# Sparsemax thresholds from Newton steps on the candidates instead of a sort, and a rolled exact loop

## What is computed

```
xn   = layernorm(x);  q = xn@Wq + bq;  k = ctx@Wk + bk;  v = ctx@Wv + bv
s    = q k^T / sqrt(32)                  # per head, 100 x 722
p    = sparsemax(s)                      # max(s - tau, 0), tau such that each row sums to 1
x1   = x + (p v)@Wo + bo
x2n  = layernorm(x1)
y    = x1 + sqrt((x2n@cos(theta+theta_noise))^2 + (x2n@sin(phi+phi_noise))^2)
```

## Time and profile before

| | us |
|---|---|
| median of 3 runs | 852.85 |
| lowest, highest | 851.33, 861.3 |
| span of the profiled execution | 858.3 |
| VectorE busy in it | 639.5 (75%) |
| TensorE busy | 681.9 (79%) |
| ScalarE busy | 480.7 (56%) |
| GpSimd busy | 195.8 (23%) |

### The profile page before, as it was taken

One profiled execution on the slowest core, in us unless ns is written; L12 is line 12 of the kernel. 1 busy time (PEld: TensorE's weight loads), 2 busy tenths in 40 slices (PEclk: granted clock), 3 DMA queues, 4 the chain that ended last, 5 costly groups with the idle time before them and its releaser, 6 DMA issues.

```text
span 858.3 us, 17053 instructions
## 1 busy us (share of the span) xinstructions
PE 681.9 (79%) x5152; PEld 441.6 (51%) x5152; DVE 639.5 (75%) x4046; ACT 480.7 (56%) x936; POOL 195.8 (23%) x147
## 2 busy tenths in 40 slices
PE   3895843879977789899889988988949898986485
PEld 3562522645555454665467455855437455742351
DVE  2799995599936997499929994799638995899401
ACT  3271754655485554875388546765537566843441
POOL 4940450001520034102520162004410053000000
PEclk9898885979989799899989999999969999998687
DMA  7620100000020000200020002000020000000000
GB/s 233 247 99 1 68 3 1 2 2 1 11 90 1 0 10 1 90 0 0 10 91 0 0 10 67 24 0 10 1 86 4 0 10 11 3 1 10 11 3 10
DMA packets 14576, 26.27 MB, mean 31 GB/s; under 512 B 2106, under 2 KB 2106, under 8 KB 14478
## 3 DMA queue, kind: packets, MB, share of 16 engines
q1 hardware_dynamic: 14478, 25.35, 8.9%
HBM read 23.71 MB, written 1.64 MB: 30 GB/s over the span
## 4 chain that ended last, share of the span: by engine, by line
DVE 71%; issue 9%; PE 7%; DMA 5%; DVEq 3%; SPq 3%; ACT 2%; ACTq 0%; POOL 0%; POOLq 0%
DVE cand L772 22%; DVE cand L784 17%; DVE top L779 14%; DMA xq<-in_x 3%; PE tps L438 3%; DVE csum L794 2%; PE work L422 2%; DMA out_y<-att 2%; DVE x L871 2%; DVE gk L797 2%; DVE topz L790 1%; DVE g_max L800 1%; SPq L197 1%; DVE st L747 1%; PE work L342 1%
## 5 line engine op out<-in xcount | busy, mean ns | idle before, releaser
L772 DVE MAX8 cand<-S 100x8 f32<-100x60 f32 (+1 forms) x1536 | 191.0, 208 | 49.0 <-ACT S L576 28.7
L438 PE MATMUL tps<-ident,S 100*128 100x100 f32 x768 | 106.0, 282 | 82.3 <-DVEq L864 47.5
L422 PE MATMUL work<-kT,qz 128*100 128x361 f16 x768 | 153.8, 342 | 0.8 <-ACT k_f L597 0.8
L613 ACT ACTIVATE S<-S,neg_tau 100x722 f32<-100x722 f32 x128 | 115.0, 900 | 68.2 <-DVE neg_tau L802 68.2
L287 POOL TENSOR_TENSOR ctxT<-ctxT_f,ctxT 128x1024 f16<-128x1024 f32 x24 | 54.0, 2248 | 426.5 <-ACT ctxT_f L576 426.5
L784 DVE MATCH_REPLACE8 cand<-top,cand 100x96 f32<-100x96 f32 x640 | 149.1, 250 | 0.0
L337 PE MATMUL work<-wv,ctxT 128*128 128x512 f16 x576 | 130.8, 384 | 19.8 <-ACT v L576 19.4
L779 DVE MAX8 top<-cand 100x8 f32<-100x96 f32 x768 | 141.2, 252 | 0.0
L438 PEld LDWEIGHTS tps<-ident,S 100*128 100x128 f32 x768 | 87.0, 158 | 104.0 <-ACT pT L576 45.5
L337 PE MATMUL work<-ctxT,wk 128*128 128x361 f16 x768 | 128.3, 329 | 10.8 <-ACT k_f L597 9.1
L576 ACT ACTIVATE S<-work 100x722 f32<-100x722 f32 x128 | 99.6, 778 | 33.0 <-PE work L422 30.8
(11 more groups left out here) (102 smaller groups left out, 671.4 us busy)
## 6 DMA issues: line engine op xcount, KB each, us to landing
ctx_nat<-in_ctx SPq DMA_DIRECT2D x8, 1280.0 KB
xq<-in_x SPq DMA_DIRECT2D x8, 200.0 KB
xr<-in_x SPq DMA_DIRECT2D x8, 200.0 KB
out_y<-att SPq DMA_DIRECT2D x8, 200.0 KB
ctx_nat<-in_ctx SPq DMA_DIRECT2D x8, 164.0 KB
wq<-in_L_xattn_Wq SPq DMA_DIRECT2D x1, 1024.0 KB, 7.4
S<-in_L_xattn_Wk SPq DMA_DIRECT2D x1, 1024.0 KB, 9.5
S<-in_L_xattn_Wv SPq DMA_DIRECT2D x1, 1024.0 KB, 11.2
```

The source lines that it names most:

```text
L422: last = nc.tensor.matmul(buf[0:L, half, 0:HALF], qz2[:, i, h // G, h % G, :], kT2[:, j, h // G, half * HALF:(half + 1) * HALF], start=(n ...
L438: last = nc.tensor.transpose(tps[:, half, c * L:(c + 1) * L], S[0:L, h, kc * P:(kc + 1) * P], ident[0:L, 0:L])
L613: nc.scalar.activation(S[0:L, h, 0:N], S[0:L, h, 0:N], ACT.Relu, bias=neg_tau[:, h:h + 1], accum_out=row_sum[:, h:h + 1]).then_inc(relu_do ...
L772: last = nc.vector.max(cand[:, j, 8 * i:8 * i + 8], S[0:L, h, cuts[i]:cuts[i + 1]])
```

## The change

`thresholds` becomes two parts. `maxes(b, g)` is a generator that issues the MAX8 of a group one by one, into one of two `cand` buffers. `sparse_tau(g, between)` takes tau by Newton steps for the four heads at once: the start is (sum of the two largest of each piece - 1)/24, which is not above the true tau; each step takes the differences of the first 4, 6, 8 and 8 ranks of each piece to tau, counts those that are not negative (as bf16 zeros and ones, halved in width by one addition before the reduce), sums the positive ones, and adds (sum - 1)/count to tau. Between its dependent operations `between(n)` issues n MAX8 of the next group, and all that are left at its end; for group 3 there are none. So group 3's MAX8 are now ahead of `tail1`. The semaphore counts are cleared once a pass.

`settle` copies the eight counts as integers and their maximum; if that isn't zero, a loop over the eight heads loads each count into a register and has one If with one `refine`, whose arrays are addressed by the loop's register. The 57 small memsets of the two tables at the start go.

```diff
-TOP = 48
 PIECES = 12
+RANKS = (4, 6, 8, 8)
 NEWTON_MAX = 28
-LOWEST = -3.0e38
...
-        cand = sb("cand", [L, G, NCAND])
-        top = sb("top", [L, G, TOP])
-        topz, csum, gk = (sb(n, [L, G, TOP]) for n in ("topz", "csum", "gk"))
-        chain0, inv_k = sb("chain0", [L, G, TOP]), sb("inv_k", [L, G, TOP])
-        g_max = sb("g_max", [L, G])
+        cand = sb("cand", [L, 2, G, NCAND])
+        dif, over = sb("dif", [L, G, NCAND]), sb("over", [L, G, NCAND], BF16)
+        tau_t, f_sum, count_g, inv_g = (sb(n, [L, G]) for n in ("tau_t", "f_sum", "count_g", "inv_g"))
+        zero = sb("zero", [L, 1])
...
-        scratch = cand[:, :, :].rearrange("p g n -> p (g n)").bitcast(BF16)[:, 0:N]
+        scratch = dif[:, :, :].rearrange("p g n -> p (g n)").bitcast(BF16)[:, 0:N]
...
-            def thresholds(b, g):
-
-                base = step = 0
-
+            def maxes(b, g):
 
                 dve.wait_ge(s_ready, H * b + G * (g + 1))
                 dve.sem_inc(scores_seen, 1)
-                dve.sem_clear(find)
-                dve.sem_clear(tau_step)
                 for j in range(G):
-                    h = G * g + j
                     for i in range(PIECES):
-                        last = nc.vector.max(cand[:, j, 8 * i:8 * i + 8], S[0:L, h, cuts[i]:cuts[i + 1]])
-                    last.then_inc(find, 1)
...
+                        last = nc.vector.max(cand[:, g % 2, j, 8 * i:8 * i + 8],
+                                             S[0:L, G * g + j, cuts[i]:cuts[i + 1]])
+                        if i == PIECES - 1:
+                            last.then_inc(found, 1)
+                        yield
+
+            def sparse_tau(g, between):
+
+                n = tau_count[0]
+                pieces = cand[:, g % 2, :, :].rearrange("p g (i r) -> p g i r", r=8)
+                dve.wait_ge(found, G * (g + 1))
+                nc.vector.tensor_reduce(f_sum[:, :], pieces[:, :, :, 0:2], mybir.AxisListType.XY,
+                                        ALU.add).then_inc(tau_step, 1)
+                between(4)
+                dve.wait_ge(tau_step, n + 1)
+                nc.vector.tensor_scalar(tau_t[:, :], f_sum[:, :], -1.0, 1.0 / (2 * PIECES), ALU.add,
+                                        ALU.mult).then_inc(tau_step, 1)
+                n += 2
+                for ranks in RANKS:
+                    E = PIECES * ranks
+                    d4 = dif[:, :, 0:E].rearrange("p g (i r) -> p g i r", r=ranks)
+                    t4 = tau_t[:, :].rearrange("p (g a c) -> p g a c", a=1, c=1)
+                    between(1)
+                    dve.wait_ge(tau_step, n)
+                    nc.vector.tensor_tensor(d4, pieces[:, :, :, 0:ranks],
+                                            t4.broadcast_to([L, G, PIECES, ranks]),
+                                            ALU.subtract).then_inc(tau_step, 1)
+                    between(1)
+                    dve.wait_ge(tau_step, n + 1)
+                    nc.vector.tensor_scalar(over[:, :, 0:E], dif[:, :, 0:E], 0.0, None, ALU.is_ge)\
+                        .then_inc(tau_step, 1)
+                    nc.vector.tensor_scalar(dif[:, :, 0:E], dif[:, :, 0:E], 0.0, None, ALU.max).then_inc(tau_step, 1)
+                    dve.wait_ge(tau_step, n + 2)
+                    nc.vector.tensor_tensor(over[:, :, 0:E // 2], over[:, :, 0:E // 2], over[:, :, E // 2:E],
+                                            ALU.add).then_inc(tau_step, 1)
+                    dve.wait_ge(tau_step, n + 3)
+                    nc.vector.reduce_sum(f_sum[:, :], dif[:, :, 0:E], AX).then_inc(tau_step, 1)
+                    dve.wait_ge(tau_step, n + 4)
+                    nc.vector.reduce_sum(count_g[:, :], over[:, :, 0:E // 2], AX).then_inc(tau_step, 1)
+                    between(1)
+                    dve.wait_ge(tau_step, n + 6)
+                    nc.vector.tensor_scalar(count_g[:, :], count_g[:, :], 1.0, None, ALU.max).then_inc(tau_step, 1)
+                    between(1)
+                    dve.wait_ge(tau_step, n + 7)
+                    nc.vector.reciprocal(inv_g[:, :], count_g[:, :]).then_inc(tau_step, 1)
+                    between(1)
+                    dve.wait_ge(tau_step, n + 8)
+                    nc.vector.scalar_tensor_tensor(f_sum[:, :], f_sum[:, :], -1.0, inv_g[:, :], ALU.add,
+                                                   ALU.mult).then_inc(tau_step, 1)
+                    between(1)
+                    dve.wait_ge(tau_step, n + 9)
+                    nc.vector.tensor_tensor(tau_t[:, :], tau_t[:, :], f_sum[:, :], ALU.add).then_inc(tau_step, 1)
+                    n += 10
+                between(1)
+                dve.wait_ge(tau_step, n)
+                nc.vector.tensor_scalar(neg_tau[:, G * g:G * (g + 1)], tau_t[:, :], -1.0, None,
+                                        ALU.mult).then_inc(tau_ready, 1)
+                tau_count[0] = n
+                between(G * PIECES)
+
+            def filler(of):
+
+                def between(n):
+                    for _ in range(n):
+                        next(of, None)
+                return between
...
             def refine(h):
 
+                p = S[0:L, bass.ds(h, 1), 0:N].rearrange("p a n -> p (a n)")
                 dve.sem_clear(fix)
-                n = newton(h, 0, row_sum[:, h:h + 1])
-                n = newton(h, n, new_sum[:, :])
+                n = newton(p, 0, row_sum[:, bass.ds(h, 1)])
+                n = newton(p, n, new_sum[:, :])
...
-                nc.vector.tensor_scalar(flag_bits[:, :], flag_ps, 0.5, None, ALU.is_gt).then_inc(check_step, 1)
-                dve.wait_ge(check_step, 1)
-                nc.vector.scalar_tensor_tensor(flag_bits[:, :], flag_bits[:, :], 1.0, bit[:, :], ALU.mult, ALU.mult,
-                                               accum_out=flag_code[:, :]).then_inc(check_step, 1)
+                nc.vector.tensor_copy(flag_i[:, :], flag_ps).then_inc(check_step, 1)
+                nc.vector.reduce_max(any_i[:, :], flag_ps, AX).then_inc(check_step, 1)
                 dve.wait_ge(check_step, 2)
-                nc.vector.tensor_copy(flag_i[:, :], flag_code[:, :]).then_inc(check_step, 1)
-                dve.wait_ge(check_step, 3)
-                todo = dve.value_load(flag_i[0:1, 0:1], min_val=0, max_val=2 ** (2 * G) - 1)
+                todo = dve.value_load(any_i[0:1, 0:1], min_val=0, max_val=L)
                 with dve.If(todo > 0):
-                    for n in range(2 * G):
-                        with dve.If((todo >> n) & 1 > 0):
-                            refine(2 * G * part + n)
+                    with dve.Fori(0, 2 * G) as n:
+                        rows = dve.value_load(flag_i[0:1, bass.ds(n, 1)], min_val=0, max_val=L)
+                        with dve.If(rows > 0):
+                            refine(n + 2 * G * part)
...
-                thresholds(b, 0)
-                thresholds(b, 1)
-                thresholds(b, 2)
+                dve.sem_clear(found)
+                dve.sem_clear(tau_step)
+                tau_count[0] = 0
+                none = filler(iter(()))
+                filler(maxes(b, 0))(G * PIECES)
+                sparse_tau(0, filler(maxes(b, 1)))
+                sparse_tau(1, filler(maxes(b, 2)))
+                sparse_tau(2, filler(maxes(b, 3)))
                 if not first:
                     tail1(b - 1)
                 mark(b, 0)
-                thresholds(b, 3)
+                sparse_tau(3, none)
                 if not first:
                     sum_squares(b - 1)
                 settle(b, 0)
```

More of the change, by code:

```diff
@@ L156, in build_kernel @@
         att_ready, x1_ready, res_ready = (sem(n) for n in ("att_ready", "x1_ready", "res_ready"))
-        find, tau_step, check_step, fix = sem("find"), sem("tau_step"), sem("check_step"), sem("fix")
         scores_seen = sem("scores_seen")
+        found, tau_step, check_step, fix = sem("found"), sem("tau_step"), sem("check_step"), sem("fix")
         ln1_stat, ln1_sd, ln1_step, xn_ready = (sem(n) for n in ("ln1_stat", "ln1_sd", "ln1_step", "xn_ready"))
@@ L758, in ln1 @@
                            ln1_stat, ln1_sd, ln1_step, xn_ready)
-            def thresholds(b, g):
-                base = step = 0
+            def maxes(b, g):
                 dve.wait_ge(s_ready, H * b + G * (g + 1))
                 dve.sem_inc(scores_seen, 1)
-                dve.sem_clear(find)
-                dve.sem_clear(tau_step)
                 for j in range(G):
-                    h = G * g + j
                     for i in range(PIECES):
-                        last = nc.vector.max(cand[:, j, 8 * i:8 * i + 8], S[0:L, h, cuts[i]:cuts[i + 1]])
-                    last.then_inc(find, 1)
[L774 to L782, removed]
-                            dve.wait_ge(find, base + n - G + j + 1)
-                            nc.vector.match_replace(cand[:, j, :], top[:, j, 8 * r:8 * r + 8], cand[:, j, :],
-                                                    LOWEST).then_inc(find, 1)
```

(27 more changed lines are left out.)

10 lines of the change are left out of this document (4 added, 6 removed).

## The result

The changed kernel takes 875.6 us (median of 4; 873.22 to 879.74), the one before 852.09 (median of 4 by now): a ratio of 1.0267, 95% interval 1.0223 to 1.031. It is slower.

A forecast was written before the change was run, and what follows sets the result against it. VectorE was taken to bound the kernel. Six steady passes +8, first pass +1.7, three flagged settles +19.5 and last pass -6.3 gave +23 us on the median 852.85: 876 us, 8-in-10 range 842 to 902.

The forecast's parts named there:

- the two paths: Steady pass: x2n to TensorE's FFN and k projections; fourth threshold to sum_squares and ScalarE's root, relus and k copies.
- Two points set the pass: VectorE, steady pass: only when x2n is out (T+54.5) and when sum_squares runs (T+71.6) matter.
- The chain's price: VectorE's new threshold chain: 11.7 us with MAX8 between, 11.2 without; a group's period 14.15 us against 16.6.
- Free MAX8: VectorE's chain: the 29 interleaved MAX8 of a group cost nothing, 19 are left, 2.35 us.
- Order: Group 1's scores delay threshold 0 to T+18.4; group 3's maxes ahead of tail1 spend the gain of three groups.
- GpSimd: Shared port pair holds VectorE's subtracts, compares, clamps, adds and updates: x2n +1.1 us, threshold 3 T+73.0 against T+71.7.
- The pass grows by 1.3 us: Steady pass: threshold 3's delay lengthens each pass by 1.3 us; six of them, +8.
- The exact loop: Settle: the same three heads are refined; each flagged settle costs +6.5 us (3 to 16), three times, +19.5.
- Rival C: Exact loop: each rolled turn stalls for code as the old Ifs did once, 36 us more, about 905; chance 0.15.
- First and last pass: First pass: chains and GpSimd +3.2 us, +1.7 with its settle; last pass: -5.0, and -1.3 for the settle.
- ten refined heads: Exact loop: four steps fail to converge for more heads, some 9 us each; ten heads 960 us; chance 0.03.
- Rival A: VectorE's chain: GpSimd meets little of it, x2n at T+52.0, pass 3.5 us shorter, 836 us; chance 0.17.

The follow-up runs named there:

- run 4: The changed kernel with tail1 moved ahead of the 19 MAX8 left of group 3: 879.3 us, 1.026 of the kernel before.
- run 8: The changed kernel with tail1 ahead of group 3's remaining MAX8 and GpSimd's qz operations behind the fourth threshold: 856.9 us, 1.008 of the kernel before.
- run 9: The changed kernel with only GpSimd's qz operations moved behind the fourth threshold, tail1 left in place: 872.0 us, 1.021 of the kernel before.
- the quiet kernel: The changed kernel with GpSimd's operand subtractions and additions for sequences 1 to 7 cut to one column: 848.8 us, 0.998 of the kernel before.
- run 7: The changed kernel without interleaving, a group's 48 MAX8 together behind the threshold of the group before: 944.7 us, one run.
- run 3: The kernel before with the new rolled exact loop and settle but the old thresholds: 852.6 us, 0.994 of the kernel before.
- run 2: The changed kernel with the old settle and unrolled exact loop, keeping the new thresholds: 868.4 us, 1.014 of the kernel before.
- run 1: The kernel before, unchanged, traced once more: 857.81 us, one run.
- run 10: The kernel before with a rolled exact loop that tests bits of a code word in a register: 845.1 us, 0.991 of the kernel before.

## Why the prediction was right, and where it was not

876 us were forecast, 875.6 measured, slower as forecast and within the range. The direction and the two paths were right; that the totals agree to 0.4 us is in part luck, as the steps show:

- **Two points set the pass**: shown by runs 4, 8 and 9. The clock in the tail is a third thing that sets it.
- **The chain's price.** Chains in the last pass, where GpSimd is idle: thresholds 14.08 us apart (14.15 forecast). The bf16 add took 250 ns for 192 elements, the fast rate; compare of f32 to bf16 342 ns (median) for 384 in the quiet kernel, the fast rate too. Free MAX8: shown by run 7.
- **Order.** Threshold 0 at T+17.8 to 18.9 (18.4): right.
- **GpSimd.** In passes 2 to 5 x2n +1.3 to 2.4 us (1.1), threshold 3 +1.7 to 2.8 (1.3): right in kind, some 0.7 us small. In passes 1 and 6, where x1 had not been held before, +3.2 to 3.4 and +3.8 to 4.0. The rule of the Trainium skill (SBUF — State Buffer, "SBUF: two separate sides") on the shared port pair agrees with every trace read here, also for GpSimd, which waited in its turn (2.32 us for 2.13 in run 3).
- **"The pass grows by 1.3 us"** is the step that failed in the traces: passes 2 to 4 changed by -1.1, -0.4 and +0.4 us, although thresholds and x2n came later by more than forecast. The step carried the delay of the fourth threshold over to the next T and so took the tail behind it as fixed. It was not: 20.6 to 21.0 us before, 18.2 to 18.3 after. Settle is 0.7 to 1.1 us of that where the clock is at 2.4 GHz on both sides (run 2's 18.84 against 18.15; run 1's 19.45 against run 10's 18.31, both with the old thresholds), and I had it on the path in the first and last pass only. The rest is TensorE's clock, which the prediction took as the same on both sides: in the first trace of the kernel before the tails of passes 2 to 4 all ran partly at 1.2 GHz, in the changed kernel's two of the three not at all. Within one kernel such a fall cost 1.2 us (run 1) and 2.3 us (run 10). With the clock at 2.4 GHz through both tails, 91.01 us before stand against 91.45 and 92.56 after, +0.4 and +1.5.
- **The exact loop**: three heads, six L808 (L832 now), right. A turn took 1.16 us (1.3 forecast), a settle 4.6 to 4.9 more (6.5): mis-sized by the turn and by the addresses made in registers, for which I took 1 us. Rival C didn't come: in the turn shown the gap behind the branch is 0.14 us, in pass 5 the longest is 0.50. But the term's other side was missed: the rolled loop alone makes the kernel faster (0.994), with a gap elsewhere that shrank and let x1 come first.
- **First and last pass**: threshold 3 of the first +2.9 us (+3.2), last pass -6.6 (-6.3).
- **Sum in the traces**: passes 1 to 6 without the settles of 1 and 5 +5.4 (forecast 8), settles +14.4 (19.5), first pass's chain +2.9, less 2.2 behind it and 0.7 ahead of it (1.7), last -6.6: 13 us, where 23 were forecast. That the medians differ by 23.5 owes 10 us to something else. Two candidates are on record: low clock in the tails of the traced execution of before (a mean granted clock of 0.900, as in its longest executions), and the x1 meeting, which its traced executions lost by 0.03 us. How the 10 us divide between them is open: to settle it, a trace of a short execution would be needed.
- **Slips in the sums.** Rival C's 36 us on top of 876 give 912, not 905; ten refined heads at 9 us each for the seven more give 939, not 960; threshold 3 of the last pass, 63.5 against 68.7, is -5.2, not -5.0. None touches the forecast by more than 0.2 us.

Rival A's time (836) is that of a GpSimd that meets nothing. The quiet kernel took 849 with one flagged settle more, and its pass 3, which holds that settle, took 102.6 us where pass 4 took 88.4: without it some 835 by my estimate from these two passes.

## What to carry to other kernels

Before replacing VectorE instructions, sort them by whether GpSimd can hold them: MAX8, MATCH_REPLACE and reduces were never held here; additions and subtractions of two arrays in SBUF, and tensor_scalar operations from SBUF to SBUF, were, and a meeting cost up to a whole GpSimd operation. A chain of some 40 short dependent operations beside GpSimd's work lost 4 to 6 us, which stand in the profile as longer operations and not as waits. Where a pass is the later of two paths, mend both or expect little. And before explaining a difference of 1 to 2 us between two passes, compare the granted clock in them.

## What the runs showed of the hardware

- An order decided by 0.03 us (x1 against GpSimd's operation) moves x2n by 1.8 us and the fourth threshold by 2.0.
- TensorE's granted clock is such a lottery too. Two passes of run 4, equal until the last relu, differed by 2.5 us by whether the clock fell again at a wait of 1.1 us; two of run 10 by 2.3 us (87.6 and 89.9).
- After the branch over eight unrolled bodies VectorE's queue did nothing for 3.2 us; after the same branch over one rolled body it went on within 0.5 us. A turn of the rolled loop with a flag's load took 1.16 us, with a bit of a register in the load's place 0.86.
